# Selective-scan stage of a fused layer: one GpSimd product for two units, six state buffers, four C rows loaded per channel tile

## The chip, the cores and the metric

The kernel is one program on one core of a Trainium2 chip. Five engines work in it side by side, each with its own instruction stream: TensorE (PE in the profile, its weight loads PEld), VectorE (DVE), ScalarE (ACT), GpSimd (POOL) and SyncE (SP), which here issues nearly all DMAs. They meet only at semaphores. The metric is the time of one execution on the device in microseconds. An engine takes its instructions strictly in the order in which they were written; whatever stands behind a waiting instruction waits with it.

## The reference, cut to what matters

```python
x = x + tanh(g_xattn[0]) * ssm(ctx_1024, layernorm(x), ...)     # stages 1 and 2
x = x + tanh(g_ffn[0]) * moe_ffn(layernorm(x), ...)             # the rest

def ssm(hidden, z, ...):                   # B=4, L=1024 steps, DI=1024 channels, DS=16 states
    ...                                    # projections, convolution, softplus: delta, B_t, C_t, u
    def step(state, xs):
        d_t, B_t, C_t, u_t = xs
        dA = exp(d_t[..., None] * A)                                # decay, per channel and state
        state = state * dA + (d_t * u_t)[..., None] * B_t[:, None, :]
        y_t = einsum('ben,bn->be', state, C_t)                      # sum over the 16 states
        return (state, y_t)
    ...
    y = (y + D * u) * silu(z)
```

The change touches only the part that runs `step` and the two lines after it.

## The kernel before, in words

The program has five stages in a row: the inputs of the state-space model (`mamba_inputs`), the scan (`selective_scan`), and three of the feed-forward part. Only the scan stage is changed.

**Tiling.** There are 4 sequences of 8 channel tiles, so 32 tiles (`NU`) of 128 channels, channels on the partitions and the 1024 time steps along the row. Each tile has 16 state indices; one state index of one tile is a *unit*, numbered k from 0 to 511, with i the tile and n = k mod 16 the state index. A *turn* is the change from one sequence to the next: then new matrices and new rows of C are loaded.

**One unit goes through five steps, in this order.**

1. TensorE, `multiply_b` (L1138): 8 matmuls of 128x128 make (delta * u) * B for the unit in PSUM (`psb`), in two halves. Each half waits until ScalarE has copied that half of the unit before out of `psb` (semaphore `s_ev`).
2. ScalarE, `copy_input` (L1061): two copies of 512 columns from `psb` to SBUF (`dbu`). ScalarE's list in unit k is: exponential of unit k (step 3), then the copies of unit k + 3 (`AHEAD`), and in state index 2 of each tile the small copy that makes the `skip` matrix (L1077).
3. ScalarE, L1069: the decay exp(delta * A) of unit k into one of two PSUM buffers `da`. It waits until the scan of unit k - 2 has ended, which frees the buffer.
4. VectorE, L1099: the scan along time (`tensor_tensor_scan`), `h` from `da` and `dbu`, 1024 columns, into one of `HR` = 4 buffers of `h`. It waits for the decay, for the copies of its group of four units, and for the ring: the sum of unit k - 4 (step 5) must be done.
5. GpSimd, L1116: `h` times the row of C, in place, 1024 columns. Then TensorE, `add_state` (L1148): 8 transposing matmuls add the unit into `psy`, the output of the tile. TensorE's list is: `multiply_b(k)`, then `add_state(k - 6)` (`BEHIND`). With state indices 6 to 9 the D * u term is added too (L1157).

**The gate.** When all 16 units of a tile are in `psy`, VectorE multiplies it by the gate (`gate_tile`, L1091). In VectorE's list that instruction stands behind the scan of state index `GATED` = 1 of the next tile. The first `add_state` of the next tile waits for it, since it overwrites `psy`.

**Loads.** All 16 rows of C of a sequence (each repeated over 128 partitions, 512 KB) stay in SBUF for its 8 tiles and are replaced at a turn. Per tile SyncE further issues, in this order: delta and A of the next tile; the store of the gated tile before and u; four quarters of `du_taps` of the next tile (four DMAs of 128 KB each; quarter r waits for `multiply_b` of unit 12 + r); silu(z).

In the text, "product of C" is the GpSimd instruction, "matrix product" is `multiply_b`, "sum" is `add_state`, and e(k) is the end of the scan of state index k, counted from the start of one tile on into the next (so 16 is state index 0 of the next tile).

Of the kernel before, what the change touches and what calls it, by code (L numbers as in the profile page):

```python
# [6 lines left out]
P = 128  # L7
# [7 lines left out]
ET = DI // P  # L15
# [29 lines left out]
def after(eng, sem, value):  # L45

    if isinstance(value, int):
        if value > 0:
            eng.wait_ge(sem, value)
    else:  # L50
        assert value.min_val > 0
        eng.wait_ge(sem, value)
# [825 lines left out]
def selective_scan(nc, io, dr, ident, arena, m0, duT, early):  # L878
# [4 lines left out]
    with ExitStack() as ctx:  # L883
# [4 lines left out]
        PARTS = 4  # L888
        CP = NC // PARTS
        CH = CP // 2  # L890
        HR = 4
        AHEAD, BEHIND = 3, 6
        GATED, SKIPPED = 1, 6
        GATED_AT = 8
        FIRST = 5
        m0, m1 = m0[:], sb("m", [P, TB * ROW], F32R)[:]
        skip = sb("skip", [P, P])
        gate = sb("gate2", [P, 1])
        m = [v.rearrange("p (t c n) -> p t c n", t=TB, c=NC) for v in (m0, m1)]
        c = sb("c", [P, NST, L])  # L900
        ad = sb("ad", [P, 2, NST + 1])
        dl = sb("dl", [P, 2, L])
        dbu = sb("dbu", [P, 2, GN, L])
# [33 lines left out]
        block = ctx.enter_context(nc.Block())  # L937
        f32 = lambda ap: ap.bitcast(F32)

        def units(body):  # L940
            for i in range(NU):
                for n in range(NST):
                    body(i, n, i * NST + n)

        @block.sync
        def _(sp):
# [21 lines left out]
                    sp.dma_start(dst_, src_).then_inc(s_m[half], 16)  # L968

            def load_c(b, n):  # L970
                after(sp, s_hc, (b * ET - 1) * NST + n + 1 if b else 0)
                sp.dma_start(c[:, n], dr["c"][b, n].partition_broadcast(P)).then_inc(s_cl[n], 16)

            def load_u(i):
                if i == 0:
# [8 lines left out]
            def store(i):  # L984
                sp.wait_ge(s_gated, i + 1)
                sp.dma_start(dr["gated"][i // ET].rearrange("(t p) (e c) -> e p t c", p=P, c=P)[i % ET], aux[:])\
                    .then_inc(s_gst if i < NU - 1 else early["gated"], 16)
# [23 lines left out]
            load_m(0, 1)  # L1011
            for n in range(FIRST, NST):
                load_c(0, n)

            for i in range(NU):
                b = (i + 1) // ET
                turn = i % ET == ET - 1 and b < B
                turned = i % ET == 0 and i
                final = i == NU - 1
                if not final:  # L1020
                    load_delta(i + 1)
                if turned:
                    for n in range(10, 12):
                        load_c(b, n)
                if i:
                    store(i - 1)
                    load_u(i)
                if turned:
                    for n in range(12, NST):
                        load_c(b, n)  # L1030
                if turn:
                    load_m(b, 0)
                    for n in range(4):
                        load_c(b, n)
                for r in range(PARTS):
                    if not final:
                        load_du(i + 1, r)
                load_silu(i)
                if final:
                    first_weights()  # L1040
                    first_tokens()
                if turn:
                    load_m(b, 1)
                    for n in range(4, 10):
                        load_c(b, n)
# [62 lines left out]
        @block.gpsimd  # L1108
        def _(pool):
            pool.memset(f32(m1), 0.0).then_inc(s_zero, 1)  # L1110

            def unit(i, n, k):
                if i % ET == 0:
                    pool.wait_ge(s_cl[n], (i // ET) * 16 + 16)
                pool.wait_ge(s_scan, k + 1)
                pool.tensor_tensor(h[:, k % HR, :], h[:, k % HR, :], c[:, n, :], ALU.mult).then_inc(s_hc, 1)  # L1116

            units(unit)

        @block.tensor  # L1120
        def _(pe):
# [19 lines left out]
            def add_state(k):  # L1141

                i, n = k // NST, k % NST
                if n == 0:
                    after(pe, s_gated, i)
                pe.wait_ge(s_hc, k + 1)
                for t in range(ET):
                    mm = pe.matmul(psy[:, t, :], h[:, k % HR, t * P:(t + 1) * P], ident[:], is_transpose=True,  # L1148
                                   start=(n == 0 and t % 4 == 0), stop=(n == NST - 1 and t % 4 == 3))
# [1059 lines left out]
```

## Time and profile before

| | us |
|---|---|
| three runs: median (lowest, highest) | 4099.43 (4098.16, 4102.16) |
| span of the profiled execution | 4099.1 |
| scan stage in it, first scan start to last gate start | 492.2 to 1725.1 |
| busy in the whole span: PE, DVE, ACT, POOL | 3803.9, 3017.5, 2141.8, 1727.5 |
| POOL products of C, 512 | 1205.3 |
| DVE scans, 512 | 1135.0 |
| ACT decays, 512, and copies, 1020 | 583.7 and 547.9 |

The profile gives one time for its execution, its span; it is 0.3 us from the median of the three runs. Busy time is the sum over instructions, and two instructions that overlap by a little at their border both count in full. Idle time is put before the instruction that ended it, with what released it: "[0.67 <-PE psy L1148]" says that the engine sat for 0.67 us until the sum at L1148 let it go on. An engine's busy share of the whole span says little here, as the stages differ; each stage has to be read by itself.

### The profile page before, as it was taken

To read this page: it belongs to the slowest core of one execution; us is meant where nothing else is said; L and a number is where in the kernel's file an instruction comes from. 1 tells how busy PE (TensorE), PEld (TensorE's weight loads), DVE (VectorE), ACT (ScalarE), POOL (GpSimd) and SP (SyncE) were. 2 spreads that over 40 slices of the span, in tenths; PEclk is the share of its full clock that TensorE was granted. 3 is DMA by queue.
4 is the path that set the end of the run, shared out by engine and by line. 5 is a ranking of instruction groups with operands and counts; after the bars stand their busy time and mean duration, and the time that the engine had idled before them with its cause. 6 is when DMAs were issued, how large, how long until landed. Compare 5 with 4: busy or idle time off the path is not lost. (4 is left out here: it accounts for less than half of the span.)

```text
span 4099.1 us, 60052 instructions
## 1 busy us (share of the span) xinstructions
PE 3803.9 (93%) x21088; PEld 3147.7 (77%) x21088; DVE 3017.5 (74%) x3711; ACT 2141.8 (52%) x2768; POOL 1727.5 (42%) x977
## 2 busy tenths in 40 slices
PE   8898588888888888799999989999999999999999
PEld 3444488788888788678888878888888888788887
DVE  7898799999999999877777755555555555455555
ACT  3688699889889989722222244444444444200000
POOL 0243299999999999823333310000000000122222
PEclk9999599999999999999999999999999999999999
DMA  6687843643643643355555656677777766677543
GB/s 236 241 294 259 299 141 114 180 140 109 185 140 110 184 140 117 132 198 179 182 187 187 222 197 236 236 240 241 237 244 239 234 235 235 221 281 267 199 164 118
DMA packets 328298, 819.60 MB, mean 200 GB/s; under 512 B 65920, under 2 KB 109696, under 8 KB 318784
## 3 DMA queue, kind: packets, MB, share of 16 engines
q1 hardware_dynamic: 296240, 750.13, 54.4%
q0 software_dynamic: 31744, 67.23, 5.5%
q8 instruction: 104, 1.70, 0.2%
q14 instruction: 66, 0.54, 0.0%
q10 hardware_dynamic: 144, 0.00, 0.0%
HBM read 603.38 MB, written 245.27 MB: 207 GB/s over the span
## 5 line engine op out<-in xcount | busy, mean ns | idle before, releaser
L1116 POOL TENSOR_TENSOR h<-h,c 128x1024 f32<-128x1024 f32 x512 | 1205.3, 2409 | 27.6 <-DVE h L1099 23.9
L1099 DVE TENSOR_TENSOR_SCAN h<-da,dbu 128x1024 f32<-128x1024 f32 x512 | 1135.0, 2272 | 50.1 <-ACT dbu L1061 28.7
L1148 PE MATMUL psy<-ident,h 128*128 128x128 f32 x4096 | 562.4, 281 | 81.6 <-POOL h L1116 60.0
L1069 ACT ACTIVATE da<-dl,ad 128x1024 f32<-128x1024 f32 x512 | 583.7, 1140 | 100.5 <-DVE h L1099 88.5
L1061 ACT ACTIVATE dbu<-psb 128x512 f32<-128x512 f32 x1020 | 547.9, 589 | 34.1 <-PE psb L1138 32.0
L1148 PEld LDWEIGHTS psy<-ident,h 128*128 128x128 f32 x4096 | 445.1, 143 | 129.6 <-POOL h L1116 90.9
L1947 POOL DMA_INDIRECT xg<-scratch_xn,ids x62 | 61.3, 989 | 1010.2 <-PE psT L1965 997.8
L2105 DVE TENSOR_TENSOR wsp<-arena,wsp 128x2048 fp32r<-128x2048 f32 x146 | 329.9, 2286 | 77.3 <-ACT wsp L2059 77.3
L1605 ACT ACTIVATE hT_s<-psH_s 128x512 fp32r<-128x512 f32 x64 | 38.2, 598 | 625.1 <-PE psH_s L1533 625.1
L1138 PE MATMUL psb<-m,du_taps 128*128 128x128 f32 x2048 | 294.0, 290 | 43.9 <-ACT dbu L1061 35.7
L1138 PEld LDWEIGHTS psb<-m,du_taps 128*128 128x128 f32 x2048 | 258.6, 193 | 79.7 <-ACT dbu L1061 73.0
L1408 POOL DMA_INDIRECT scratch_tab<-tok_s,si_s x128 | 131.2, 1025 | 425.5 <-DVE si_s L1746 384.1
L1138 PE MATMUL psb<-m_first,du_taps 128*128 128x128 f32 x2032 | 286.4, 289 | 21.1 <-DMA du_taps<-scratch_duT 9.9
L1138 PEld LDWEIGHTS psb<-m_first,du_taps 128*128 128x128 f32 x2032 | 254.2, 196 | 28.8 <-DMA du_taps<-scratch_duT 14.2
L2059 ACT ACTIVATE wsp<-arena 128x2048 fp32r<-128x2048 f32 x146 | 271.8, 1914 | 2.1 <-DMA arena<-in_w 1.9
L479 PE MATMUL psX<-arena 128*128 128x512 f32 x512 | 229.0, 599 | 12.1 <-DMA arena<-in_ctxT 12.1
L1459 PE MATMUL psO_s<-wsp,hT_s 128*128 128x512 f32 x512 | 202.9, 396 | 5.2 <-DVE hT_s L1644 5.2
L1460 PE MATMUL psO_s<-wsp,hT_s 128*128 128x512 f32 x512 | 200.1, 391 | 0.0
L1461 PE MATMUL psO_s<-wsp,hT_s 128*128 128x512 f32 x512 | 200.0, 391 | 0.0
L2064 ACT ACTIVATE ob<-psO 128x512 f32<-128x512 f32 x64 | 38.2, 597 | 301.3 <-PE psO L1976 301.3
L479 PEld LDWEIGHTS psX<-arena 128*128 128x128 f32 x512 | 95.8, 193 | 120.9 <-issue 107.9
L1658 DVE SCALAR_TENSOR_TENSOR ac_s<-arena,weights,ac_s 128x1024 f32<-128x1024 f32 x128 | 164.3, 1283 | 13.3 <-DVE ac_s L1658 0.2
(232 smaller groups left out, 8253.8 us busy)
## 6 DMA issues: line engine op xcount, KB each, us to landing
arena<-in_w SPq DMA_DIRECT2D x192, 1024.0 KB, 6.1
du_taps<-scratch_duT SPq DMA_DIRECT2D x496, 128.0 KB, 2.9
c<-scratch_c SPq DMA_DIRECT2D x64, 512.0 KB, 12.5
scratch_xT<-xT_s SPq DMA_DIRECT2D x32, 1024.0 KB, 4.8
scratch_ob<-ob SPq DMA_DIRECT2D x64, 512.0 KB, 2.9
xT_place<-scratch_xT SPq DMA_DIRECT2D x32, 1024.0 KB, 6.3
scratch_duT<-duT SPq DMA_DIRECT2D x52, 512.0 KB, 4.2
xz<-in_x SPq DMA_DIRECT2D x32, 512.0 KB, 5.4
```

The lines of the kernel that those rows point to most:

```text
L479: mm = pe.matmul(psX[q % 2][:, hb * HB:(hb + 1) * HB], w_in[:, k, et * P:(et + 1) * P], ctxT[:, b % 2, k, hb * HB:(hb + 1) * HB], start=(k ...
L1061: act.activation(dbu[:, g % 2].rearrange("p n (t c) -> p n t c", c=NC)[:, :, :, c0:c0 + CH], product_bank(k)[:, half * CH:(half + 1) * CH] ...
L1069: act.activation(da[k % 2][:, :], dl[:, i % 2, :], ACT.Exp, scale=ad[:, i % 2, n:n + 1]).then_inc(s_da, 1)
L1099: dve.tensor_tensor_scan(h[:, k % HR, :], da[k % 2][:, :], dbu[:, (k // GN) % 2, k % GN, :], 0.0, ALU.mult, ALU.add).then_inc(s_scan, 1)
L1116: pool.tensor_tensor(h[:, k % HR, :], h[:, k % HR, :], c[:, n, :], ALU.mult).then_inc(s_hc, 1)
L1138: mm = pe.matmul(product_bank(k)[:, j], duT[:, r * CP + j, :], m[g // 2][:, :, r * CP + j, g % 2 * GN:(g % 2 + 1) * GN], start=True, stop= ...
L1148: mm = pe.matmul(psy[:, t, :], h[:, k % HR, t * P:(t + 1) * P], ident[:], is_transpose=True, start=(n == 0 and t % 4 == 0), stop=(n == NST ...
L1459: pe.matmul(dst, l[0], r[0], start=(n == 0), stop=False)
L1460: pe.matmul(dst, l[0], r[1], start=False, stop=False)
L1461: mm = pe.matmul(dst, l[1], r[0], start=False, stop=(n == len(lhs) - 1))
L2059: act.activation(wsp[slot][:, 0, halves[half]], raw[:, c, halves[half]], ACT.Copy).then_inc(s_whi, 1)
L2105: dve.tensor_tensor(wsp[slot][:, 1, halves[half]], raw[:, c, halves[half]], f32(wsp[slot][:, 0, halves[half]]), ALU.subtract).then_inc(s_w ...
```

## The change

Two units of neighbouring state indices become a pair. GpSimd multiplies both by their rows of C in one instruction over 2048 columns. For that the two states and the two rows of C must lie side by side: the ring of states grows from 4 to 6 buffers, and C shrinks from 16 to 14 rows. State indices 14 and 15 share the place of 6 and 7, and these four rows are loaded anew in every tile (`stream_c`). `BEHIND` goes from 6 to 8 and `GATED` from 1 to 2.

```diff
--- before.py
+++ after.py
@@ -888,16 +888,18 @@
         PARTS = 4
         CP = NC // PARTS
         CH = CP // 2
-        HR = 4
-        AHEAD, BEHIND = 3, 6
-        GATED, SKIPPED = 1, 6
+        HR = 6
+        AHEAD, BEHIND = 3, 8
+        GATED, SKIPPED = 2, 6
+        PAIR = 2
+        SHARED = (6, 14)
         GATED_AT = 8
         FIRST = 5
         m0, m1 = m0[:], sb("m", [P, TB * ROW], F32R)[:]
         skip = sb("skip", [P, P])
         gate = sb("gate2", [P, 1])
         m = [v.rearrange("p (t c n) -> p t c n", t=TB, c=NC) for v in (m0, m1)]
-        c = sb("c", [P, NST, L])
+        c = sb("c", [P, NST - PAIR, L])
         ad = sb("ad", [P, 2, NST + 1])
         dl = sb("dl", [P, 2, L])
         dbu = sb("dbu", [P, 2, GN, L])
@@ -937,6 +939,12 @@
         block = ctx.enter_context(nc.Block())
         f32 = lambda ap: ap.bitcast(F32)
 
+        def c_place(n):
+
+            return n if n < SHARED[1] else n - SHARED[1] + SHARED[0]
+
+        streamed = [n + j for n in SHARED for j in range(PAIR)]
+
         def units(body):
             for i in range(NU):
                 for n in range(NST):
@@ -968,8 +976,16 @@
                     sp.dma_start(dst_, src_).then_inc(s_m[half], 16)
 
             def load_c(b, n):
-                after(sp, s_hc, (b * ET - 1) * NST + n + 1 if b else 0)
-                sp.dma_start(c[:, n], dr["c"][b, n].partition_broadcast(P)).then_inc(s_cl[n], 16)
+                if n not in streamed:
+                    after(sp, s_hc, ((b * ET - 1) * NST + n) // PAIR + 1 if b else 0)
+                    sp.dma_start(c[:, n], dr["c"][b, n].partition_broadcast(P)).then_inc(s_cl[n], 16)
+
+            def stream_c(i, first):
+
+                before = i * NST + first - NH
+                after(sp, s_hc, before // PAIR + 1 if before >= 0 else 0)
+                for n in range(first, first + PAIR):
+                    sp.dma_start(c[:, c_place(n)], dr["c"][i // ET, n].partition_broadcast(P)).then_inc(s_cl[n], 16)
 
             def load_u(i):
                 if i == 0:
@@ -1011,6 +1027,8 @@
             load_m(0, 1)
             for n in range(FIRST, NST):
                 load_c(0, n)
+                if n == SHARED[0]:
+                    stream_c(0, n)
 
             for i in range(NU):
                 b = (i + 1) // ET
@@ -1023,6 +1041,7 @@
                     for n in range(10, 12):
                         load_c(b, n)
                 if i:
+                    stream_c(i, SHARED[0])
                     store(i - 1)
                     load_u(i)
                 if turned:
@@ -1035,6 +1054,8 @@
                 for r in range(PARTS):
                     if not final:
                         load_du(i + 1, r)
+                    if r == 2:
+                        stream_c(i, SHARED[1])
                 load_silu(i)
                 if final:
                     first_weights()
@@ -1110,10 +1131,16 @@
             pool.memset(f32(m1), 0.0).then_inc(s_zero, 1)
 
             def unit(i, n, k):
-                if i % ET == 0:
+                if n in streamed:
+                    pool.wait_ge(s_cl[n], i * 16 + 16)
+                elif i % ET == 0:
                     pool.wait_ge(s_cl[n], (i // ET) * 16 + 16)
-                pool.wait_ge(s_scan, k + 1)
-                pool.tensor_tensor(h[:, k % HR, :], h[:, k % HR, :], c[:, n, :], ALU.mult).then_inc(s_hc, 1)
+                if n % PAIR == PAIR - 1:
+                    pool.wait_ge(s_scan, k + 1)
+                    first = (k - PAIR + 1) % HR
+                    states = h[:, first:first + PAIR, :].rearrange("p a l -> p (a l)")
+                    rows = c[:, c_place(n) - PAIR + 1:c_place(n) + 1, :].rearrange("p a l -> p (a l)")
+                    pool.tensor_tensor(states, states, rows, ALU.mult).then_inc(s_hc, 1)
 
             units(unit)
 
@@ -1143,7 +1170,7 @@
                 i, n = k // NST, k % NST
                 if n == 0:
                     after(pe, s_gated, i)
-                pe.wait_ge(s_hc, k + 1)
+                pe.wait_ge(s_hc, k // PAIR + 1)
                 for t in range(ET):
                     mm = pe.matmul(psy[:, t, :], h[:, k % HR, t * P:(t + 1) * P], ident[:], is_transpose=True,
                                    start=(n == 0 and t % 4 == 0), stop=(n == NST - 1 and t % 4 == 3))
```

**VectorE's list.** Its first rows in the scan stage, before:

```order
L1083 UNCONDITIONAL_BRANCH
L1099 SCALAR_TENSOR_TENSOR h<-da,dbu 128x1024 x18
L1091 SCALAR_TENSOR_TENSOR aux<-psy,gate,aux 128x1024
L1099 SCALAR_TENSOR_TENSOR h<-da,dbu 128x1024 x16
L1091 SCALAR_TENSOR_TENSOR aux<-psy,gate,aux 128x1024
```

and now:

```order
L1104 UNCONDITIONAL_BRANCH
L1120 SCALAR_TENSOR_TENSOR h<-da,dbu 128x1024 x19
L1112 SCALAR_TENSOR_TENSOR aux<-psy,gate,aux 128x1024
L1120 SCALAR_TENSOR_TENSOR h<-da,dbu 128x1024 x16
L1112 SCALAR_TENSOR_TENSOR aux<-psy,gate,aux 128x1024
```

(The scans carry the name of their instruction class here.) The gate of a tile stands one scan later.

**TensorE's list**, in the second tile, from the sum of state index 6 (the one followed by the first D * u rows, L1157) to that of 10. `m` is the matrix of state indices 8 to 15, `m_first` that of 0 to 7. Before:

```order
L1148 MATMUL psy<-ident,h 128x128 x8
L1157 MATMUL psy<-skip,aux 128x128 x2
L1138 MATMUL psb<-m,du_taps 128x128 x8
L1148 MATMUL psy<-ident,h 128x128 x8
L1157 MATMUL psy<-skip,aux 128x128 x2
L1138 MATMUL psb<-m,du_taps 128x128 x8
L1148 MATMUL psy<-ident,h 128x128 x8
L1157 MATMUL psy<-skip,aux 128x128 x2
L1138 MATMUL psb<-m,du_taps 128x128 x8
L1148 MATMUL psy<-ident,h 128x128 x8
L1157 MATMUL psy<-skip,aux 128x128 x2
L1138 MATMUL psb<-m_first,du_taps 128x128 x8
```

and now:

```order
L1175 MATMUL psy<-ident,h 128x128 x8
L1184 MATMUL psy<-skip,aux 128x128 x2
L1165 MATMUL psb<-m,du_taps 128x128 x8
L1175 MATMUL psy<-ident,h 128x128 x8
L1184 MATMUL psy<-skip,aux 128x128 x2
L1165 MATMUL psb<-m_first,du_taps 128x128 x8
L1175 MATMUL psy<-ident,h 128x128 x8
L1184 MATMUL psy<-skip,aux 128x128 x2
L1165 MATMUL psb<-m_first,du_taps 128x128 x8
L1175 MATMUL psy<-ident,h 128x128 x8
L1184 MATMUL psy<-skip,aux 128x128 x2
L1165 MATMUL psb<-m_first,du_taps 128x128 x8
```

The first matrix product of the next tile stands behind the sum of state index 9 before and of 7 now: each sum has two more matrix products ahead of it. The sum of state index 15 stands behind the matrix product of 23 instead of 21.

**SyncE's list** of one ordinary tile, before:

```order
L950 DMA dl<-scratch_dl 128x1024
L951 DMA ad<-scratch_a 128x17
L986 DMA scratch_gated<-aux 128x8x128
L978 DMA aux<-scratch_u 128x1024
L958 DMA du_taps<-scratch_duT 32x1024 x16
L982 DMA aux<-scratch_szT 128x1024
```

and now:

```order
L958 DMA dl<-scratch_dl 128x1024
L959 DMA ad<-scratch_a 128x17
L988 DMA c<-scratch_c 128x1024 x2
L1002 DMA scratch_gated<-aux 128x8x128
L994 DMA aux<-scratch_u 128x1024
L966 DMA du_taps<-scratch_duT 32x1024 x12
L988 DMA c<-scratch_c 128x1024 x2
L966 DMA du_taps<-scratch_duT 32x1024 x4
L998 DMA aux<-scratch_szT 128x1024
```

Two rows of C stand ahead of the store, two between the third and the fourth quarter of `du_taps`. At a turn, 12 rows of C are loaded by the old path instead of 16.

## Rows read from the trace of the kernel before

**Rows 1.** The page: span, and two of the costliest groups.
```profile
span 4099.1 us, 60052 instructions
...
L1116 POOL TENSOR_TENSOR h<-h,c 128x1024 f32<-128x1024 f32 x512 | 1205.3, 2409 | 27.6 <-DVE h L1099 23.9
L1099 DVE TENSOR_TENSOR_SCAN h<-da,dbu 128x1024 f32<-128x1024 f32 x512 | 1135.0, 2272 | 50.1 <-ACT dbu L1061 28.7
```

**Rows 2.** Timeline of GpSimd, merged: start, length, instruction, count.
```profile
1158.79 264.49 POOL L1116 TENSOR_TENSOR h<-h,c 128x1024 f32<-128x1024 f32 x112 [0.81 <-DVE h L1099]
```

**Rows 3.** Timeline of VectorE in the scan stage; in brackets the idle time before.
```profile
1155.25 1.26 DVE L1091 SCALAR_TENSOR_TENSOR aux<-psy,gate,aux 128x1024 f32<-128x1024 f32 x1
...
1499.51 31.23 DVE L1099 TENSOR_TENSOR_SCAN h<-da,dbu 128x1024 f32<-128x1024 f32 x14
1530.88 4.47 DVE L1099 TENSOR_TENSOR_SCAN h<-da,dbu 128x1024 f32<-128x1024 f32 x2
1536.03 1.28 DVE L1091 SCALAR_TENSOR_TENSOR aux<-psy,gate,aux 128x1024 f32<-128x1024 f32 x1 [0.67 <-PE psy L1148]
1537.23 31.21 DVE L1099 TENSOR_TENSOR_SCAN h<-da,dbu 128x1024 f32<-128x1024 f32 x14
...
1725.09 1.28 DVE L1091 SCALAR_TENSOR_TENSOR aux<-psy,gate,aux 128x1024 f32<-128x1024 f32 x1 [5.11 <-PE psy L1148]
```

**Rows 4.** Timeline of all engines around one gate.
```profile
1534.83 1.09 PE L1148 MATMUL psy<-ident,h 128*128 128x128 f32 x8 [0.40 <-POOL h L1116]
...
1535.54 1.12 ACT L1069 ACTIVATE da<-dl,ad 128x1024 f32<-128x1024 f32 x1
1535.68 1.10 PE L1138 MATMUL psb<-m_first,du_taps 128*128 128x128 f32 x8
...
1539.54 1.12 ACT L1069 ACTIVATE da<-dl,ad 128x1024 f32<-128x1024 f32 x1 [1.89 <-DVE h L1099]
...
1541.23 1.16 PE L1138 MATMUL psb<-m,du_taps 128*128 128x128 f32 x8 [0.60 <-ACT dbu L1061]
...
1542.22 1.06 PE L1148 MATMUL psy<-ident,h 128*128 128x128 f32 x8
```

**Rows 5.** Groups of GpSimd: count, then busy us and mean ns.
```profile
L1110 POOL MEMSET m<- 128x8192 f32 x1 | 7.0, 6970 | 89.2 <-POOLq L89 89.2
L865 POOL MEMSET m_first<- 128x4096 f32 x1 | 3.5, 3512 | 1.7 <-PE psX L479 1.7
...
L1402 POOL TENSOR_TENSOR tok_s<-tok_s,token_step_s 128x1 int32<-128x1 int32 x30 | 6.4, 213 | 0.0
```

**Rows 6.** Timeline of TensorE after two stalls at turns.
```profile
791.18 1.12 PE L1138 MATMUL psb<-m_first,du_taps 128*128 128x128 f32 x8 [2.05 <-DMA du_taps<-scratch_duT]
792.13 1.06 PE L1148 MATMUL psy<-ident,h 128*128 128x128 f32 x8
...
1100.70 1.12 PE L1138 MATMUL psb<-m_first,du_taps 128*128 128x128 f32 x8 [1.76 <-DMA du_taps<-scratch_duT]
1101.65 1.89 PE L1148 MATMUL psy<-ident,h 128*128 128x128 f32 x8
1103.19 1.95 PE L1138 MATMUL psb<-m_first,du_taps 128*128 128x128 f32 x8
```

**Rows 7.** Windows: length, busy of five engines, granted clock, DMA share, GB/s.
```profile
1101.00:1105.00 4.00, 4.00 (x25) 4.00 (x24) 3.33 (x2) 2.70 (x4) 4.00 (x3) 0.59 1.05 248
```

**Rows 8.** Timeline of SyncE: the 16 loads of du_taps of one tile.
```profile
1246.15 10.42 SPq L958 DMA_DIRECT2D du_taps<-scratch_duT  x16
```

**Rows 9.** DMA view at the first turn (810 to 850): size, median us to landing.
```profile
c<-scratch_c SPq DMA_DIRECT2D x4, 512.0 KB, 6.7
du_taps<-scratch_duT SPq DMA_DIRECT2D x16, 128.0 KB, 7.3
```

**Rows 10.** The same view over the whole scan stage.
```profile
du_taps<-scratch_duT SPq DMA_DIRECT2D x496, 128.0 KB, 2.9
```

**Rows 11.** Timeline of GpSimd: its first instruction behind the scan stage.
```profile
1729.89 2.35 POOL L1383 TENSOR_TENSOR arena<-arena 128x1024 f32<-128x1024 f32 x1 [6.05 <-DMA arena<-in_x]
```

## The prediction

> **What bounds the kernel now.** I read the page first, then the timelines of single engines inside the scan stage, because the change is there alone. On the page the product of C has 512 instructions of 2409 ns and almost no idle time before them, 27.6 us in all; the scans have 512 of 2272 ns and 50.1 us idle [rows 1]. So two engines are nearly full. The timeline of GpSimd shows how full: 112 products without a gap in 264.49 us, 2.362 us each, so a tile of 16 takes 37.78 us [rows 2]. VectorE's timeline has the same period from gate to gate with a little air in it: 14 scans in 31.2 us are 2.23 us each, 16 of them 35.67; the gate takes 1.20 until the next scan starts; and it waits 0.67 for the last sum [rows 3]. 35.67 + 1.20 + 0.67 is 37.54, and 0.14 lies before the scan that starts at 1530.88; tiles around have up to 0.2 more. GpSimd sets the pace, VectorE's own work is only 36.87, and everything that a faster GpSimd can give is the difference: 0.9 us in each tile, 28 us in all. That is the ceiling of the gain. Whether it is reached depends on the wait at the gate, which stands on VectorE's path.
>
> **What the change does at the gate.** The gate needs the sum of state index 15. What that sum waits for is in TensorE's list, and there the change puts two more matrix products ahead of it. I follow them back with durations of the trace, counting from e(17), the end of the scan of state index 1 of the next tile.
>
> - Before, the sum of 15 waits for GpSimd only: it starts at 1534.83 behind an idle 0.40 put down to the product of C, ends at 1535.92, and the gate starts 0.11 later [rows 3, 4]. Matrix product 21, ahead of it, had long been possible.
> - Now matrix product 23 stands ahead of it. That needs the copy of 22 out of `psb`, and the copy of 22 stands behind the decay of 19 on ScalarE, which waits for e(17). In the tile shown e(17) is 1530.88 + 4.47 = 1535.35 and the decay of 19 starts at 1535.54, behind the copy for `skip` [rows 3, 4]: 0.19.
> - From the start of a decay to the matrix product that its copies release: 1539.54 to 1541.23 is 1.69. From there to the sum behind it, 1542.22, is 0.99, and the sum takes 1.06 [rows 4]. Then 0.11 to the gate.
> - Sum: the gate can start at e(17) + 0.19 + 1.69 + 0.99 + 1.06 + 0.11 = e(17) + 4.04. The change moves the gate one scan later, so VectorE is free for it at e(17) + 2.23. It waits 1.81 us. Neither GpSimd's speed nor the larger ring changes that.
>
> VectorE's period is then at least 35.67 + 1.20 + 1.81 + 0.14 = 38.82 us. Against the 37.78 of now each tile loses 1.0. This is a new wait in the place of the one removed: 0.67 becomes 1.81.
>
> **What a pair costs on GpSimd.** No instruction of 2048 columns with two inputs is in the trace. If nothing fixed is saved, the pair takes 2 x 2.362 = 4.72. If an instruction's fixed part is what one element takes, 213 ns, it takes 4.51. If the fixed part is what the two fills give, 2 x 3512 - 6970 = 54 ns, it takes 4.67 [rows 2, 5]. I take 4.55, near the first, since the 213 is of the same operation, though of another type; a few tens of ns of it are already hidden at the border of two products. Below 4.60 it doesn't set the pace, as shown next; above it does.
>
> GpSimd now has a chain of its own around the gate. The pair (14, 15) ends; the sum of 14 starts 0.06 later, matrix product 23 follows 0.85 on (1534.83 to 1535.68), the sum of 15 about 1.0 behind that and ends 1.09 later, 0.11 to the gate, 1.20, and the scan of 19 takes 2.23, before which the pair (18, 19) can't start; in that time only the pair (16, 17) is done. So a period is 7 pairs and 6.6 us [rows 3, 4]. With 4.55 it is 38.5, below VectorE's 38.82: hidden. The two meet at 4.60. With 4.67 it is 39.3, with 4.72 it is 39.6.
>
> The Trainium skill (GPSIMD Engine Reference, "Elementwise: side-by-side cycle accounting") gives 4497 ns for this operation at 2048 fp32 columns. The trace has only the 1024-column form; taking the page's figure as an estimate, the period of 7 pairs would be 38.1, the pace stays VectorE's and the sum stays as it is; it only lowers the chance of the first rival.
>
> **The other parts.**
> - Ring of six: the scan k + 6 needs the sum of k, which by the same chain ends near e(k + 2) + 3.9, while that scan can start at e(k + 5), 2.8 us later. No stall, no gain.
> - TensorE behind the gate: its next matrix product (25) waits for the decay of 21, which waits for the first scan behind the gate. The sum of 16 ends 1.1 us behind the gate; 25 starts 2.23 + 0.08 + 1.69 = 4.0 behind it. TensorE idles 2.8 us in each tile, where at the gate shown it now idles 0.60 [rows 4]. After a stall of 1.76 the granted clock was 0.59 over 4 us and a group of 8 matmuls took 1.89 and 1.95 instead of 1.09; after one of 2.05 it stayed at 1.06 [rows 6, 7]. At that clock two groups cost 1.7 us more. The sums have the 2.8 us of the ring to hide it in, the copies for the next group of four scans about 1.5; I take 0.1 per tile, with 0 and 0.6 as ends.
> - Loads: four rows of C per tile, 2 MB. Two at the pair's end, needed three pairs and the gate later, some 15 us; 6.7 us was their landing even at a turn [rows 9]. Two between the third and fourth quarter of `du_taps`. Matrix product 12, which lets the first quarter go, ends at e(6) + 0.08 + 1.69 + 1.1 = e(6) + 2.9. SyncE needs 10.42 us for the 16 issues, 0.65 each [rows 8], and the two rows of C 1.3 more: the last is issued at e(6) + 14.6 and lands 2.9 later [rows 10], at e(6) + 17.5. Matrix product 19 wants it at e(13) + 1.77, which is e(6) + 17.4; about 1 us of slack lies in the copies behind it. I take 0; bounds 0 and 1.0 (at a turn the landing was 7.3 [rows 9]).
> - Turns: 12 rows of C instead of 16, two of the missing ones replaced by streamed ones. I take -1 for each of three, ends -3 and +3.
> - End: the last sum comes some 2 us later, but the next stage waits for its own load until 1729.89, 3.5 us behind the last gate's end [rows 3, 11]: nothing. Start: the first pair waits one scan more, +1.
>
> **The sum.** 31 gates stand inside VectorE's list. At 24 of them there was a wait like the 0.67; at 7, near the start and the turns, there was none, as at 1155.25 [rows 3]. 24 x 1.04 + 7 x 1.81 = 25 + 13 = 38. Clock 31 x 0.1 = 3. Turns -3, start +1. Together +39 on the profiled 4099.1, which stands 0.3 us under the median of the runs: 4138 us. With the lower ends (copy stall before each tile gone, turns -3 each, clock 0) it is +26, with the upper (clock 0.6, loads at a third of their bound) about +64.
>
> **Rivals.**
> 1. *GpSimd still sets the pace*: the pair saves little, 4.67 to 4.72. Periods of 39.3 to 39.6 are 31 x 1.5 to 1.9 = 47 to 58, 4150 to 4160 with the rest. For it: the fill's fixed part is only 54 ns. Against: 213 ns for one element. Chance 0.17.
> 2. *The clock falls behind each gate and the loss isn't hidden*: 0.9 to 1.7 us in each tile on top, 31 x 0.9 = 28 to 31 x 1.7 = 53, 4163 to 4188. For it: 1.89 and 1.95 after a stall shorter than the new one. Against: slack, and the stall of 2.05 without a fall [rows 6]. The Trainium skill (TensorE: Matmul & The Clock Gate, "HAM oscillation") says that idle gaps repeated in each period of a loop can throttle the clock once per period; only the rows of one of two stalls here agree. Chance 0.08.
> 3. *Faster: the gate's wait goes away.* This needs the sum of 15 done by e(18), so that the decay of 19 and its copies are no part of its path. Then VectorE's own 36.87 + 0.14 is the period, 0.77 less: 31 x 0.77 = 24, 4075 us. Against it stands the fixed list of TensorE. It decides from the point where the sum of 15 ends before e(17) + 2.1; I get 3.9. Chance 0.06.
> 4. *No difference*: part of the wait is hidden, e.g. the copies before each tile no longer stall and turns give back 3 us each. Period within 0.25 of now, 4091 to 4107. Chance 0.07.
> 5. *Loads of `du_taps` late in each tile*, 1 us: 31 more, 4165. Chance 0.05.
>
> The forecast keeps 0.57. A difference under 0.2%, 8 us, can't be told from none here. Slower: 0.57 + 0.17 + 0.08 + 0.05 = 0.87; same 0.07; faster 0.06. The range 4112 to 4168 holds the forecast, rival 1, rival 5 and the near part of rival 2.
>
> **What would show it.** In the profile after: GpSimd has 256 products and an idle of about 2 us before the pair behind each gate; the pair's length reads off directly (4.5 to 4.6 expected). VectorE waits about 1.8 us before each gate, released by the sum, and little elsewhere; gates are 38.8 apart. TensorE waits before matrix product 23 for ScalarE's copies, not for GpSimd, and again some 2.8 us after the gate; the granted clock there shows rival 2. I am wrong if the wait before the gate is under 1 us, or if TensorE's wait ahead of the last sum is released by GpSimd.

## The result, and the profile after

| | median us (lowest, highest; runs) | against before, 95% interval |
|---|---|---|
| before, run beside it | 4098.8 (4096.4, 4102.2; 4) | |
| after | 4283.0 (4273.2, 4291.7; 4) | 1.0449 [1.0434, 1.0465] |
| forecast | 4138, range 4112 to 4168 | |

The change costs 184 us where 39 were forecast. The sign and the place were right; the size was not, and the time lies outside the range. The page of the changed kernel, five of its rows:

```profile
span 4283.7 us, 59932 instructions
...
L1143 POOL TENSOR_TENSOR h<-h,c 128x2048 f32<-128x2048 f32 x256 | 1167.6, 4601 | 252.9 <-DVE h L1120 249.9
L1120 DVE TENSOR_TENSOR_SCAN h<-da,dbu 128x1024 f32<-128x1024 f32 x512 | 1131.9, 2271 | 172.2 <-issue 94.1
...
L1165 PE MATMUL psb<-m_first,du_taps 128*128 128x128 f32 x2032 | 336.3, 319 | 131.5 <-DMA du_taps<-scratch_duT 119.6
...
c<-scratch_c SPq DMA_DIRECT2D x176, 512.0 KB, 5.7
```

GpSimd's work shrank from 1205.3 to 1167.6 us, as meant, but it now idles 252.9 us, not 27.6, waiting for scans [rows 1]. The scans themselves take what they took; their idle time rose from 50.1 to 172.2. The idle time before the 32 gates rose from 22.6 to 91.2. These two, 122 and 69, less 3 us that the scans are shorter in sum, are all of the difference and 3 us more. So VectorE says where the time went. Its timeline over one tile after, to be held against [rows 3]:

```profile
1599.84 6.65 DVE L1120 TENSOR_TENSOR_SCAN h<-da,dbu 128x1024 f32<-128x1024 f32 x3 [5.38 <-ACT dbu L1082]
1609.53 1.28 DVE L1112 SCALAR_TENSOR_TENSOR aux<-psy,gate,aux 128x1024 f32<-128x1024 f32 x1 [3.04 <-PE psy L1175]
1610.73 11.00 DVE L1120 TENSOR_TENSOR_SCAN h<-da,dbu 128x1024 f32<-128x1024 f32 x5
1622.89 17.74 DVE L1120 TENSOR_TENSOR_SCAN h<-da,dbu 128x1024 f32<-128x1024 f32 x8 [1.16 <-ACT dbu L1082]
1643.27 6.66 DVE L1120 TENSOR_TENSOR_SCAN h<-da,dbu 128x1024 f32<-128x1024 f32 x3 [2.64 <-issue]
1652.09 1.28 DVE L1112 SCALAR_TENSOR_TENSOR aux<-psy,gate,aux 128x1024 f32<-128x1024 f32 x1 [2.17 <-PE psy L1175]
```

Three waits are to be seen, by their brackets: one before the row of 3 scans (state indices 0 to 2 of the next tile), one before the gate, one before the row of 8 (indices 8 to 15). Over the 28 intervals between gates from 585 to 1828 us the first is 1.39 to 5.94, 3.65 in the mean. The gate's is 1.86 to 3.23, 2.7 in the mean. The third is 1.0 to 1.4 in 20 of the 28 and at most 0.3 in the other 8. Gates of ordinary tiles are 44.2 apart (median; 37.8 before). Only the second of these waits had been forecast, at 1.81.

"issue" in the fifth row names nobody; who it was is found on the engine that feeds the copies. The timeline of TensorE after, at the gate of 1609.53 and at the wait of 1643.27:

```profile
1610.87 1.09 PE L1175 MATMUL psy<-ident,h 128*128 128x128 f32 x8 [0.31 <-DVE aux L1112]
1614.73 1.97 PE L1165 MATMUL psb<-m,du_taps 128*128 128x128 f32 x8 [2.77 <-ACT dbu L1082]
1616.50 1.93 PE L1175 MATMUL psy<-ident,h 128*128 128x128 f32 x8
...
1640.77 1.78 PE L1165 MATMUL psb<-m_first,du_taps 128*128 128x128 f32 x8 [2.88 <-DMA du_taps<-scratch_duT]
1642.34 1.93 PE L1175 MATMUL psy<-ident,h 128*128 128x128 f32 x8
```

The matrix product at 1640.77 is number 19, the first to need the fourth quarter of `du_taps`. It waits 2.88 us for that load, and the scan of index 0, which needs the copies of all its group of four, starts 2.5 us after it. SyncE's timeline around the same loads, against [rows 8]:

```profile
1623.85 7.46 SPq L966 DMA_DIRECT2D du_taps<-scratch_duT  x12
1631.35 1.06 SPq L988 DMA_DIRECT2D c<-scratch_c  x2
1632.45 2.36 SPq L966 DMA_DIRECT2D du_taps<-scratch_duT  x4
```

The DMA view of 1623.8 to 1631.3 (12 loads, size, median us from issue to landing):

```profile
du_taps<-scratch_duT SPq DMA_DIRECT2D x12, 128.0 KB, 2.9
```

and of 1632.4 to 1635, the four loads behind the rows of C:

```profile
du_taps<-scratch_duT SPq DMA_DIRECT2D x4, 128.0 KB, 5.6
```

The issues come nearly when they were forecast: the last ends at 1634.81, 15.3 us behind e(6), where 14.6 was worked out. The landing does not. The same 128 KB take 2.9 us ahead of the two rows of C, as in [rows 10], and 5.6 behind them. The windows of 1633 to 1635 (columns as in [rows 7]) have the DMA engines full:

```profile
1633.00:1634.00 1.00, 1.00 (x12) 1.00 (x10) 1.00 (x1) 0.90 (x2) 1.00 (x1) 1.00 1.05 266
1634.00:1635.00 1.00, 1.00 (x12) 1.00 (x11) 1.00 (x2) 0.88 (x1) 1.00 (x1) 1.00 0.95 250
```

Three of the waits from 530 to 1700 us, that is over most of the scan stage (us in total, times, longest):

```profile
PE psb L1165 <- DMA du_taps<-scratch_duT: 103.6, 32, 5.1
PE psb L1165 <- ACT dbu L1082: 85.3, 62, 2.8
...
DVE aux L1112 <- PE psy L1175: 73.0, 27, 3.2
```

Over the same stretch of the kernel before, the first was 9.9 us in 15 times, the second 37.2 in 89, with 1.1 as its longest, and the last 17.5 in 24.

### The profile page after: what moved, and what is told of

The parts are those of the page before. It is cut to its first block and busy times, and to the rows that moved or that the text cites. A ratio compares the mean times of both kernels' runs of the same rounds, so it can differ in the third digit from the quotient of the medians.

```text
span 4283.7 us, 59932 instructions
## 1 busy us (share of the span) xinstructions
PE 3894.2 (91%) x21088; PEld 3282.8 (77%) x21088; DVE 3016.7 (70%) x3711; ACT 2146.0 (50%) x2768; POOL 1689.9 (39%) x721
## 5 line engine op out<-in xcount | busy, mean ns | idle before, releaser
L1143 POOL TENSOR_TENSOR h<-h,c 128x2048 f32<-128x2048 f32 x256 | 1167.6, 4601 | 252.9 <-DVE h L1120 249.9
L1120 DVE TENSOR_TENSOR_SCAN h<-da,dbu 128x1024 f32<-128x1024 f32 x512 | 1131.9, 2271 | 172.2 <-issue 94.1
L1082 ACT ACTIVATE dbu<-psb 128x512 f32<-128x512 f32 x1020 | 561.7, 595 | 187.5 <-PE psb L1165 184.7
L1175 PE MATMUL psy<-ident,h 128*128 128x128 f32 x4096 | 619.2, 301 | 15.5 <-DVE aux L1112 9.9
L1175 PEld LDWEIGHTS psy<-ident,h 128*128 128x128 f32 x4096 | 504.3, 156 | 21.8 <-DVE aux L1112 14.5
L1165 PE MATMUL psb<-m_first,du_taps 128*128 128x128 f32 x2032 | 336.3, 319 | 131.5 <-DMA du_taps<-scratch_duT 119.6
L1165 PE MATMUL psb<-m,du_taps 128*128 128x128 f32 x2048 | 336.4, 317 | 103.0 <-ACT dbu L1082 99.1
L1165 PEld LDWEIGHTS psb<-m_first,du_taps 128*128 128x128 f32 x2032 | 302.4, 226 | 150.5 <-DMA du_taps<-scratch_duT 128.1
L1165 PEld LDWEIGHTS psb<-m,du_taps 128*128 128x128 f32 x2048 | 301.0, 221 | 126.6 <-ACT dbu L1082 120.4
L1435 POOL DMA_INDIRECT scratch_tab<-tok_s,si_s x128 | 131.0, 1024 | 426.2 <-DVE si_s L1773 369.6
```

The lines of the kernel that those rows point to most:

```text
L1082: act.activation(dbu[:, g % 2].rearrange("p n (t c) -> p n t c", c=NC)[:, :, :, c0:c0 + CH], product_bank(k)[:, half * CH:(half + 1) * CH] ...
L1120: dve.tensor_tensor_scan(h[:, k % HR, :], da[k % 2][:, :], dbu[:, (k // GN) % 2, k % GN, :], 0.0, ALU.mult, ALU.add).then_inc(s_scan, 1)
L1143: pool.tensor_tensor(states, states, rows, ALU.mult).then_inc(s_hc, 1)
L1165: mm = pe.matmul(product_bank(k)[:, j], duT[:, r * CP + j, :], m[g // 2][:, :, r * CP + j, g % 2 * GN:(g % 2 + 1) * GN], start=True, stop= ...
```

## The experiments

My theory after the result: two causes, each in every tile. (A) The two rows of C that stand between the quarters of `du_taps` hold up the last quarter, which costs the first wait and part of the others. (B) The gate's place, one scan ahead of where the sum chain is done, costs the second wait and, through TensorE's idle gap and its clock, the third. The rivals: GpSimd's pair sets the pace; SyncE's issue time, not the bytes, makes the quarter late.

| run | edit | median us (lowest, highest; runs) | ratio [95%] | gate to gate, ordinary tile |
|---|---|---|---|---|
| before | | 4099.3, 4098.4, 4099.7 in the three sets | | 37.77 |
| after | | 4283.0 | 1.0449 | 44.19 |
| e1_rows_last | rows of C behind all quarters | 4173.2 (4161.4, 4175.3; 4) | 1.0176 [1.0156, 1.0196] | 39.75 |
| e2_gate_later | gate one scan later | 4203.1 (4197.7, 4213.2; 4) | 1.0264 [1.0247, 1.0281] | 40.74 |
| e3_both | e1 and e2 | 4103.2 (4100.8, 4108.5; 10) | 1.0012 [1.0002, 1.0022] | 36.79 |
| e4_small_rows | same issues, 1/16 of the bytes | 4167.3 (1) | one run | 39.71 |
| e5_two_products | e3 with two products for a pair | 4119.8 (4118.2, 4122.7; 4) | 1.0052 [1.0036, 1.0067] | 37.58 |
| e6_behind7 | e1 with `BEHIND` 7 | 4194.8 (4182.9, 4213.0; 4) | 1.0234 [1.0204, 1.0264] | 40.63 |
| e7_turn_order | e3, other order of loads at turns | 4096.2 (4091.9, 4098.0; 11) | 0.9993 [0.9984, 1.0002] | 36.77 |
| e8_before_gate2 | before with the gate one scan later | 4124.1 (4119.5, 4128.8; 4) | 1.0064 [1.0049, 1.0080] | 38.01 |
| e9_spread | e7, loads at turns spread | 4101.2 (4097.4, 4109.8; 11) | 1.0008 [0.9999, 1.0017] | 36.77 |

**e1_rows_last.**

```diff
                         load_du(i + 1, r)
-                    if r == 2:
-                        stream_c(i, SHARED[1])
+                stream_c(i, SHARED[1])
                 load_silu(i)
```

> The two rows of C for state indices 14 and 15 are issued behind all four quarters of du_taps instead of between the third and the fourth. Theory A (the last quarter is late because 1 MB of C stands ahead of it in the DMA queue): the wait of about 3.9 us before the scan of state index 0 falls under 0.5, TensorE no longer drops its clock there, the wait at the gate falls from 2.7 to about 1.9; 31 tiles x 4.5 us less, 4135 to 4155 us, that is near my first forecast. Rival B (the gap of TensorE behind the gate and the low clock it brings are the cause, and the late quarter only follows from them): the wait before state index 0 stays over 2 us, time over 4220 us.

Measured: 110 us of the 184 are gone. The waits fell as theory A says, but the time is 18 us above its range. VectorE's timeline:

```profile
943.45 6.65 DVE L1119 TENSOR_TENSOR_SCAN h<-da,dbu 128x1024 f32<-128x1024 f32 x3 [0.19 <-issue]
951.97 1.30 DVE L1111 SCALAR_TENSOR_TENSOR aux<-psy,gate,aux 128x1024 f32<-128x1024 f32 x1 [1.86 <-PE psy L1174]
953.17 11.02 DVE L1119 TENSOR_TENSOR_SCAN h<-da,dbu 128x1024 f32<-128x1024 f32 x5
964.56 17.75 DVE L1119 TENSOR_TENSOR_SCAN h<-da,dbu 128x1024 f32<-128x1024 f32 x8 [0.37 <-ACT dbu L1081]
...
990.98 1.28 DVE L1111 SCALAR_TENSOR_TENSOR aux<-psy,gate,aux 128x1024 f32<-128x1024 f32 x1 [1.85 <-PE psy L1174]
992.18 11.00 DVE L1119 TENSOR_TENSOR_SCAN h<-da,dbu 128x1024 f32<-128x1024 f32 x5
1004.27 6.65 DVE L1119 TENSOR_TENSOR_SCAN h<-da,dbu 128x1024 f32<-128x1024 f32 x3 [1.08 <-ACT dbu L1081]
```

The first wait is gone (0.19, as before the change) and the gate's is 1.86, close to the forecast 1.81: with this one disturbance out, the forecast's gate shows itself undisturbed. e(17) is 943.45 + two scans of 2.22 = 947.88, and the gate starts 4.09 later; 4.04 was worked out. Over the scan stage the scans' idle time fell from 172.2 to 77.1 and the gates' from 91.2 to 72.6, together 114, as much as the profiled spans differ; the medians differ by 110. TensorE's wait for the load, from 530 to 1700 us:

```profile
PE psb L1164 <- DMA du_taps<-scratch_duT: 22.4, 8, 5.2
```

The third wait stays, 0.37 here and 1.08 in the next tile; over the 31 tiles behind a gate it is 0.1 to 1.7, 0.8 in the mean, where it was 0.1 before the change. Its cause is in TensorE's timeline:

```profile
957.18 1.76 PE L1164 MATMUL psb<-m,du_taps 128*128 128x128 f32 x8 [2.77 <-ACT dbu L1081]
958.74 1.93 PE L1174 MATMUL psy<-ident,h 128*128 128x128 f32 x8
```

and in the windows of the gap, the stretch behind it, and the next:

```profile
955.50:957.10 1.60, 0.00 (x0) 0.00 (x0) 1.60 (x1) 1.60 (x3) 1.56 (x1) 1.00 0.32 100
957.10:960.30 3.20, 3.12 (x16) 3.12 (x17) 3.20 (x3) 3.08 (x6) 3.20 (x2) 0.55 0.49 166
960.30:963.00 2.70, 2.70 (x24) 2.70 (x23) 2.70 (x2) 2.36 (x4) 2.70 (x1) 0.90 0.02 6
```

TensorE idled 2.77 us (2.8 forecast), and the granted clock went from 1.00 to 0.55, close to the lower of its two levels, 1.2 GHz of 2.4. Two groups of 8 matmuls took 1.76 and 1.93 us instead of 1.15 and 1.06, and part of a third was slow. The Trainium skill (TensorE: Matmul & The Clock Gate, "HAM oscillation") says that idle gaps repeated in every round of a loop can throttle the clock once per round. By that rule the trace agrees: the clock fell in or just behind this gap in all 31 tiles, and the granted clock of the stage is 0.92 here and 0.86 after, 0.99 before. How long it stayed low decides the wait: in the 16 tiles in which it was low for longer the scan of index 8 waited 0.9 to 1.7 us, in the other 15 at most 0.4.

**e2_gate_later.**

```diff
-        GATED, SKIPPED = 2, 6
+        GATED, SKIPPED = 3, 6
```

> The gate moved one scan further back (GATED 3), loads as in the changed kernel. If the wait at the gate is the fixed chain decay of 19, copy of 22, matrix product 23, sum of 15, it falls from 2.7 to under 0.6 us, and the gap of 2.8 us on TensorE behind the gate and with it the 1.1 us before the scan of state index 8 go too; the late quarter stays. 31 x 3.2 us less: 4175 to 4195 us. If instead GpSimd's lag or the clock sets the gate's wait, it stays over 1.5 us and the time over 4230.

Measured: 80 us are gone; the time is 8 us above the range. Three rows of its waits, from 530 to 1700 us as above:

```profile
PE psb L1165 <- DMA du_taps<-scratch_duT: 115.4, 35, 7.5
...
PE psb L1165 <- ACT dbu L1082: 45.7, 96, 1.0
...
DVE aux L1112 <- PE psy L1175: 8.1, 23, 0.4
```

The gate no longer waits (8.1 us in all against 73.0), which the chain of the prediction says too: VectorE reaches a gate behind the scan of state index 3 at e(17) + 4.46, later than 4.04. TensorE's gap goes as well: its longest wait for the copies is 1.0 in place of 2.8. The wait for `du_taps` stays: the scan of index 0 still waits 3.2 us in the mean (3.65 after the change). The wait for the scan of index 8 is back at 0.1 us, so it belongs to the gate's gap, and the two causes are separate but for some 10 us.

**e3_both.** Both edits, and nothing else.

> Both of the edits above. If the two waits are separate and all that stands between this kernel and its engines' own work, the period of a tile is VectorE's 36.9 us plus some tenths: 4072 to 4090 us, faster than the kernel before the change. If a new wait takes their place (pairs of GpSimd at 8 x 4.55 = 36.4 us are as close behind), the period stays at 38 or more: 4110 or more.

Measured: 4103.2, so the two edits together take away 180 of the 184 us; 110 and 80 singly add up to 190. The time is in neither of the two ranges. Two tiles of VectorE's timeline, then a turn:

```profile
998.21 1.26 DVE L1111 SCALAR_TENSOR_TENSOR aux<-psy,gate,aux 128x1024 f32<-128x1024 f32 x1
999.39 26.68 DVE L1119 TENSOR_TENSOR_SCAN h<-da,dbu 128x1024 f32<-128x1024 f32 x12
1026.24 8.83 DVE L1119 TENSOR_TENSOR_SCAN h<-da,dbu 128x1024 f32<-128x1024 f32 x4 [0.17 <-issue]
1034.99 1.26 DVE L1111 SCALAR_TENSOR_TENSOR aux<-psy,gate,aux 128x1024 f32<-128x1024 f32 x1
...
1072.93 22.30 DVE L1119 TENSOR_TENSOR_SCAN h<-da,dbu 128x1024 f32<-128x1024 f32 x10
1102.17 2.29 DVE L1119 TENSOR_TENSOR_SCAN h<-da,dbu 128x1024 f32<-128x1024 f32 x1 [6.93 <-PE psy L1174]
```

In an ordinary tile VectorE now hardly waits; gates are 36.79 apart, about the 36.87 of its own work that was called the ceiling. That is 1.0 us better than before, over the 31 intervals between gates 30 us. But the kernel isn't faster, so the turns must have given it back. Two tiles across a turn, less two ordinary ones, cost 15.5, 15.3 and 15.7 us in e3; before, 7.5, 4.8 and 3.0. That is 31 us back. The row that starts at 1102.17 shows where; TensorE's row there:

```profile
1098.34 1.97 PE L1164 MATMUL psb<-m_first,du_taps 128*128 128x128 f32 x8 [7.76 <-DMA du_taps<-scratch_duT]
```

As the lists stand, the gate two scans later than before frees the buffer for u and the store two scans later, and behind those in SyncE's list wait the matrices, 2 MB of C and `du_taps`.

**e4_small_rows.**

```diff
                 for n in range(first, first + PAIR):
-                    sp.dma_start(c[:, c_place(n)], dr["c"][i // ET, n].partition_broadcast(P)).then_inc(s_cl[n], 16)
+                    w = L // 16 if first == SHARED[1] and i else L
+                    sp.dma_start(c[:, c_place(n), 0:w], dr["c"][i // ET, n, 0:w].partition_broadcast(P)).then_inc(s_cl[n], 16)
```

> As the changed kernel, but the two rows of C for state indices 14 and 15 load only 64 of their 1024 columns in all tiles but the first (the rest of the computation works on stale rows). Same DMAs, same waits, same number of issues, a sixteenth of the bytes. Theory A (bytes ahead in the queue): the wait before state index 0 falls under 0.6 us, 4135 to 4160 us. Rival C (SyncE's time to issue the two DMAs, or its wait for GpSimd ahead of them, holds the last quarter back): no change, 4260 or more.

This kernel leaves out 15/16 of the two rows in all tiles but the first and multiplies by stale numbers there, so its output is wrong and it serves for its time alone. Measured, one run: 4167.3, the time of e1 (4161.4 to 4175.3), with the rows still issued between the quarters. Its row for the load, from 530 to 1700 us:

```profile
PE psb L1166 <- DMA du_taps<-scratch_duT: 25.3, 15, 5.8
```

25.3 us as against 22.4 in e1 and 103.6 after. So it is the bytes ahead in the DMA queue that make the quarter late, not SyncE's time for two more issues (1.06 us in its rows after the change) or its wait ahead of them, both of which e4 has too.

**e5_two_products.** Against e3:

```diff
-                    states = h[:, first:first + PAIR, :].rearrange("p a l -> p (a l)")
-                    rows = c[:, c_place(n) - PAIR + 1:c_place(n) + 1, :].rearrange("p a l -> p (a l)")
-                    pool.tensor_tensor(states, states, rows, ALU.mult).then_inc(s_hc, 1)
+                    for j in range(PAIR):
+                        product = pool.tensor_tensor(h[:, first + j, :], h[:, first + j, :], c[:, c_place(n) - PAIR + 1 + j, :], ALU.mult)
+                    product.then_inc(s_hc, 1)
```

> The kernel with rows last and GATED 3, but GpSimd multiplies the two units of a pair in two instructions of 1024 columns, the second of which signals. Theory (the one instruction of 2048 columns saves 0.16 us per pair and GpSimd is as close behind VectorE as 36.5 to 36.8 us): GpSimd sets the pace again at 8 x 4.72 = 37.8 us per tile, 1.0 us more in 28 ordinary tiles: 4128 to 4140 us. Rival (the gain of the ordinary tile came from the place of the gate and the larger ring, not from the instruction): within 8 us of 4103.

Measured: 16.6 us above e3, between the two ranges: 8 us under the theory's and 9 above the rival's. The tile is 37.58, near GpSimd's 16 x 2.355 = 37.7. Its timeline is one row, 25 products at 2.355 each:

```profile
992.54 58.87 POOL L1141 TENSOR_TENSOR h<-h,c 128x1024 f32<-128x1024 f32 x25
```

and that of e3 has 8 pairs at 4.56:

```profile
1003.93 36.50 POOL L1142 TENSOR_TENSOR h<-h,c 128x2048 f32<-128x2048 f32 x8 [0.31 <-DVE h L1119]
```

So one instruction for two units is worth 2 x 2.355 - 4.56 = 0.15 us a pair, and 0.8 us per tile where GpSimd sets the pace. That is what the change can bring in an ordinary tile.

**e6_behind7.** Against e1:

```diff
-        AHEAD, BEHIND = 3, 8
+        AHEAD, BEHIND = 3, 7
```

> Rows last, GATED 2 as in the changed kernel, but BEHIND 7: the sum of state index 15 stands behind matrix product 22 instead of 23, whose copy needs the scan before. If the wait at the gate is that chain, it falls from 1.86 us to what GpSimd's own chain leaves, 0.5 to 1.5 us, and the period from about 39.5 to 38.5 to 39: 4140 to 4170 us against 4173. If a matrix product that now waits behind a sum for GpSimd starves ScalarE in every pair, the time rises over 4200.

Measured: 22 us above e1, and in neither range. It shortens the gate's chain by one matrix product, and the gate's wait falls (36.5 us in all, 60.7 in e1, both from 530 to 1700 us), but another takes its place:

```profile
PE psy L1174 <- POOL h L1142: 186.8, 151, 3.7
```

Both units of a pair are ready only at its end. One place fewer between a matrix product and its sum makes TensorE wait for the pair 151 times in some 29 tiles of 8 pairs, two pairs in three, and the next matrix product stands behind that. It is the case that the expectation put over 4200.

**e7_turn_order.** Against e3, at turns only:

```diff
                     stream_c(i, SHARED[0])
+                    if turn:
+                        load_m(b, 0)
                     store(i - 1)
...
-                if turn:
-                    load_m(b, 0)
-                    for n in range(4):
-                        load_c(b, n)
                 for r in range(PARTS):
...
                 stream_c(i, SHARED[1])
+                if turn:
+                    for n in range(4):
+                        load_c(b, n)
                 load_silu(i)
```

> The kernel with rows last and the gate at GATED 3, and at the three turns the loads in another order: the new m_first ahead of the store and of u, the first four rows of C behind the four quarters of du_taps and the two streamed rows. Theory (what that kernel lost against the kernel before stands at the turns: 15.5 us extra in each of three turns where it was 5.1, since m_first and 2 MB of C stand ahead of du_taps in one DMA queue and start only behind the gate, which is now two scans later): the stall of TensorE on du_taps of 7.8 us falls under 3, each turn loses 6 to 10 us less, time 4072 to 4086 us, faster than before by 0.3 to 0.7%. Rival (the DMA engines are full there whatever the order, and the stall moves to m, u or C): 4095 or more.

Measured: 4096.2, 7 us under e3, and not to be told from before (the interval holds 1): the rival's case. Turns cost 11.5, 9.9 and 12.8. TensorE's wait moved to the other matrix:

```profile
807.23 1.97 PE L1165 MATMUL psb<-m,du_taps 128*128 128x128 f32 x8 [4.98 <-DMA m<-scratch_bT]
```

**e8_before_gate2.** The kernel before with one number changed:

```diff
-        GATED, SKIPPED = 1, 6
+        GATED, SKIPPED = 2, 6
```

> The kernel before the change with only GATED 2 instead of 1. VectorE's wait at the gate of 0.7 us goes, but GpSimd has no gap there and sets the period of 37.78 us: within 8 us of 4099. If VectorE's wait was part of what set the pace, 31 x 0.5 us less, about 4083.

Measured: 26 us slower, a miss. A gate that is later is no gain of its own. Two rows of its waits:

```profile
PE psy L1148 <- DVE aux L1091: 67.3, 30, 2.7
...
DVE h L1099 <- ACT dbu L1061: 52.3, 54, 2.3
```

The next tile's first sum waits for the gate 67.3 us in all, against 18.4 before, and the matrix products behind it, the copies and then the scans are late. In e3 the gate stands one scan later still, and that wait is 12.4 us; by TensorE's list the reason is `BEHIND` = 8, which puts two more matrix products ahead of that sum. No run changes `BEHIND` alone.

**e9_spread.** Against e7, the four rows of C one behind each quarter, and the second matrix ahead of silu:

```diff
                         load_du(i + 1, r)
+                    if turn:
+                        load_c(b, r)
                 stream_c(i, SHARED[1])
                 if turn:
-                    for n in range(4):
-                        load_c(b, n)
+                    load_m(b, 1)
                 load_silu(i)
...
                 if turn:
-                    load_m(b, 1)
                     for n in range(4, 10):
```

> The kernel with the new order of loads at turns, in which a turn still loses 11.7 us: now the first four rows of C are issued one behind each quarter of du_taps, where the DMA engines are only two thirds busy, and the new m right behind the streamed rows, ahead of silu and all other rows. Theory (the order in the queue decides what comes late; the DMA time itself would fit): the wait of 5 us for m goes, a turn loses 6 to 9 us, time 4084 to 4092 us, faster than the kernel before by 0.2 to 0.4%. Rival (over a turn the DMA engines are full, so one wait takes the place of the other): 4093 to 4100 us.

Measured: 4101.2, no better than e3 and near the rival's range. Turns cost 13.5, 12.9 and 13.8. The wait for rows of C over the scan stage, the longest of them at the first turn, and the window of that turn:

```profile
POOL h L1143 <- DMA c<-scratch_c: 35.0, 6, 11.4
```

```profile
765.00:802.00 37.00, 30.60 (x223) 28.60 (x221) 30.04 (x14) 27.38 (x39) 26.61 (x6) 0.86 0.96 224
```

The DMA share is 0.96 over a whole tile. Three orders of the same loads gave three places for the wait: `du_taps` in e3, `m` in e7, C in e9. That suggests that the turn in e3 is short of DMA time and not of a better order. No run shows that by itself, and the kernel before had nearly the same load there (0.90 over 765 to 804) and lost less. How much of the turn belongs to the later start and how much to the queue is open.

## Why the prediction was wrong

**The failed step is the term "Loads".** It took 0, between 0 and 1.0 us per tile, from "the last is issued at e(6) + 14.6 and lands 2.9 later [rows 10], at e(6) + 17.5". The issue time nearly held: in the tile shown e(6) is 1610.73 + 4 x 2.20 = 1619.5, and the last issue ends 15.3 later. The landing was 5.6 us instead of 2.9, because 2.9 was measured with nothing large ahead in the queue. I counted the two rows of C by SyncE's time, 1.3 us, and not by their 1 MB. [Rows 9] held the warning, 7.3 us for the same 128 KB at a turn behind rows of C, and I used it only as a bound of something that happens at turns. The slack was about what I took for it: in e1, where matrix product 19 is in time, the scan of index 0 starts 1.62 us after its end, and after the change, where it is late, 0.72. That is 0.9, and about as much was lost again as the product itself ran at the lower clock, 1.97 us in place of 1.09 in most tiles. Measured price: 110 us (e1), of which the forecast had none. This is rival 5's mechanism, priced there at 1 us per tile; the wait was 3.65.

**The clock's term was too small.** It took 0.1 per tile with 0.6 as its end, 3 us in all. The gap of TensorE was right (2.77 against 2.8), but the clock fell with it in every tile, not in one case of two as in [rows 6]. In e1, with the loads out of the way, the scans of index 8 waited 26 us in the 31 tiles, 22 more than before. Ordinary tiles were 39.75 and not 37.77, over 31 intervals 61 us, where the gates' 38 and the clock's 3 were forecast: 20 too few, nearly all of it this term. That is rival 2's mechanism at 0.7 us per tile, a little under its 0.9 to 1.7. The slack that I set against it, 1.5 us for the copies, nearly covers two slow groups at 0.6 to 0.9 us more each and a part of a third, as in the tile shown with its 0.37. In the 16 tiles with the longer wait three groups and a part of a fourth ran slow, some 2.8 us.

**The turns** were taken at -1 each. After the change they cost 4.3, 3.4 and 3.2 more than ordinary tiles (7.5, 4.8 and 3.0 before), but the ordinary tiles had lost so much that this says little. In e1, with most of that loss gone, they cost 12.4, 6.0 and 4.8, 8 us more in all than before, where -3 was forecast. 20 and 11 make 31, and e1 lies 35 us above the forecast; the other 4, at the start and the end of the stage, are not taken apart.

**The gate was right.** The chain e(17) + 4.04 was 4.09 in e1, the wait 1.86 against 1.81, and where the gate was moved behind 4.04 (e2, e3) the wait vanished. Rival 3, that the wait might go away by itself, did not come true, as the prediction had argued. After the change it is larger, 2.7, since TensorE comes to the gate late and slow from the wait for the load.

**The pair was right, and so rival 1 fell.** 4.55 was taken; 8 pairs in a row took 36.50, 4.56 each. The mean record is 4601 ns, since records that touch overlap a little and both count in full. The Trainium skill (GPSIMD Engine Reference, "Elementwise: side-by-side cycle accounting") gives 4497 ns for a `tensor_tensor` addition of this width; 4.56 us is 1.4% above that, and the measurement decides. e3's tile of 36.79 also shows that GpSimd at this pace stays below VectorE's.

Together: what is left in e1, the gate's wait, the clock behind it and the turns, is 74 us where 39 were forecast, and 110 come from two loads in the wrong place. What the turns lose, and why, stays open in part.

## What to carry to other kernels

A load's time to landing belongs to what stands ahead of it in the queue: for each transfer that a change inserts, add its bytes to the landing of every small load behind it (here 2.9 us became 5.6 behind 1 MB), and look up the worst landing in the trace, not the median. A gap that a change opens in TensorE in every round of a loop is to be priced with the clock falling each time (here in 31 tiles of 31). When ordinary tiles gain and the whole does not, subtract the ordinary tile from the special ones: here, in e3, 30 us were won in 31 intervals between gates and 31 lost at three turns.

## What the hardware showed that I had not expected

- With a gap of 2.77 us in each tile the granted clock fell in every tile of e1, in some still within the gap and in others when work had resumed. In the tile shown it was 1.00 in the gap, 0.55 in the 3.2 us behind it and 0.90 in the next 2.7. Before, a gap of 2.05 had left it alone and one of 1.76 had not [rows 6].
- DMA engines that are full move very different amounts. At a share of about 1.0 the windows around C rows and `du_taps` show 250 and 266 GB/s; in e3 four windows of 5 us from 1080 to 1100, all with a share of 1.00 to 1.05, show 131, 272, 307 and 234.
- A product of 2048 columns is cheaper than two of 1024 by 0.15 us, about three times the 54 ns that the two fills give [rows 5].
